# A gated feed-forward kernel: the low halves of the second weight chunk are made on TensorE and copied out by ScalarE

## The reference, cut to what matters

```python
# x (8, 512, 512), cond (8, 128), up_w (4096, 512), down_w (512, 2048), all float32
scale = cond @ norm_w.T + 1.0
ms = jnp.mean(x * x, axis=-1, keepdims=True)
h = x * (scale[:, None, :] * jax.lax.rsqrt(ms + EPS))
u = h @ up_w.T
val, gate = jnp.split(u, 2, axis=-1)
h = val * jax.nn.gelu(gate, approximate=False)
hq = act_quant(h)       # 127 / max|h| of each row, round, clip
wq = weight_quant(down_w)   # ternary, one scale
y = hq @ wq.T
return y + x
```

## Time and profile before

| | |
|---|---|
| median of 3 runs | 813.84 us (813.39 to 815.17) |
| profiled execution | 815.42 us; its span, first to last instruction, 813.6 us |
| TensorE busy | 773.3 us, 95% of the span |
| VectorE, ScalarE, GpSimd busy | 74%, 55%, 31% of the span |
| granted TensorE clock, mean | 0.981 of full |

### The profile page before, as it was taken

How to read it: one execution, slowest core, us unless ns; L and a number is a source line. 1 busy time by engine, 2 the same in 40 slices (tenths; PEclk the granted TensorE clock), 3 DMA queues, 4 the chain that set the end, 5 groups by cost and what they waited for, 6 DMA issues and landing times.

```text
span 813.6 us, 17562 instructions
## 1 busy us (share of the span) xinstructions
PE 773.3 (95%) x6401; PEld 637.2 (78%) x6401; DVE 603.5 (74%) x855; ACT 444.0 (55%) x1023; POOL 252.9 (31%) x314
## 2 busy tenths in 40 slices
PE   5898989899899999999999999999999999999987
PEld 4687878778668897789868887789778987888853
DVE  5897987869456895489756995489647995589577
ACT  5687767477533654355535655366535654455523
POOL 3876965357211232123211223123211232111100
PEclk9799999999899999999999999999999999999999
DMA  6435763836445154535455255525645345515512
GB/s 217 158 124 182 251 215 129 318 106 222 153 182 195 56 194 147 186 118 176 169 172 180 90 180 168 183 75 184 202 129 180 113 157 187 188 46 187 185 52 78
DMA packets 34507, 130.88 MB, mean 161 GB/s; under 512 B 3224, under 2 KB 3744, under 8 KB 34464
## 3 DMA queue, kind: packets, MB, share of 16 engines
q1 hardware_dynamic: 33920, 130.04, 47.1%
q10 hardware_dynamic: 544, 0.27, 0.1%
HBM read 110.89 MB, written 19.40 MB: 160 GB/s over the span
## 4 chain that ended last, share of the span: by engine, by line
PE 71%; DVE 6%; DMA 2%; ACT 1%; issue 1%; SPq 0%; DVEq 0%; ACTq 0%
PE A L1062 11%; PE A L1065 11%; PE A L1064 11%; PE Y L1114 11%; PE B L1065 8%; PE B L1062 8%; PE B L1064 8%; DVE h L843 2%; DMA xin<-in_x_dram 2%; PE X L1010 1%; DVE mpart L822 1%; DMA w_scratch<-wslots 1%; DVE h L809 1%; PE X L1102 1%; DVE q L848 1%
## 5 line engine op out<-in xcount | busy, mean ns | idle before, releaser
L1062 PE MATMUL A<-xT,wslots 128*128 (+1 forms) x1024 | 281.3, 275 | 15.5 <-ACT snapC L599 12.2
L1065 PE MATMUL A<-xT,wslots 128*128 (+1 forms) x1024 | 281.5, 275 | 0.0
L1064 PE MATMUL A<-xT,wslots 128*128 (+1 forms) x1024 | 281.4, 275 | 0.0
L496 POOL TENSOR_TENSOR snapC<-snapC 128x256 f32<-128x256 f32 x128 | 101.9, 796 | 494.6 <-ACT snapC L599 494.2
L1062 PE MATMUL B<-xT,wslots 128*128 (+1 forms) x768 | 210.7, 274 | 0.7 <-DVE h L803 0.7
L1064 PE MATMUL B<-xT,wslots 128*128 (+1 forms) x768 | 210.7, 274 | 0.0
L1065 PE MATMUL B<-xT,wslots 128*128 (+1 forms) x768 | 210.6, 274 | 0.0
L809 DVE SCALAR_TENSOR_TENSOR h<-h,c_all,g 128x512 f32<-128x512 f32 (+1 forms) x128 | 106.6, 833 | 127.0 <-ACT g L622 126.3
L1062 PEld LDWEIGHTS A<-xT,wslots 128*128 128x128 f16 x1024 | 100.8, 98 | 32.2 <-ACT snapC L599 14.1
L1064 PEld LDWEIGHTS A<-xT,wslots 128*128 128x128 f16 x1024 | 100.9, 99 | 14.7
L1065 PEld LDWEIGHTS A<-xT,wslots 128*128 128x128 f16 x1024 | 101.0, 99 | 12.4
(11 more groups left out here) (136 smaller groups left out, 936.9 us busy)
## 6 DMA issues: line engine op xcount, KB each, us to landing
wslots<-w_scratch SPq DMA_DIRECT2D x84, 896.0 KB, 4.7
w_scratch<-wslots SPq DMA_DIRECT2D x12, 896.0 KB, 4.6
wst<-in_L_cond_up_w_dram SPq DMA_DIRECT2D x16, 512.0 KB, 5.7
xin<-in_x_dram SPq DMA_DIRECT2D x8, 1024.0 KB, 7.3
dwb<-in_L_cond_down_w_dram SPq DMA_DIRECT2D x16, 512.0 KB, 4.6
wst<-in_x_dram SPq DMA_DIRECT2D x28, 256.0 KB, 5.5
out_dram<-wst SPq DMA_DIRECT2D x28, 256.0 KB, 5.1
xin<-in_x_dram SPq DMA_DIRECT2D x4, 256.0 KB, 4.0
```

The costliest lines, as they stand in the source:

```text
L496: pool.tensor_tensor(snapC[:, s % 2, 0:H], snapC[:, s % 2, 0:H], snapC[:, s % 2, H:T], ALU.add)\
L1062: pe.matmul(into, high, xh, start=(start and kp == 0), stop=False, skip_group_check=not start)
L1064: pe.matmul(into, high, xl, start=False, stop=False, skip_group_check=not start)
L1065: mm = pe.matmul(into, low, xh, start=False, stop=last, skip_group_check=not start)
```

## The change

The low halves of chunk 1 (S2 and S4) are now made the way those of chunk 0 were: `subtract_high(s+1, 1)` on TensorE, `w_low_first(s+1, 1)` on ScalarE, and VectorE's `w_low(s+1, 1)` is gone. The semaphores count accordingly: `wlo0_ready` now rises twice for each step and `wlo_ready` two times instead of three. No DMA, tile or bank is added.

```diff
-            def w_low_first(p):
+            def w_low_first(p, c):
-                act.wait_ge(wlo_psum, p + 1)
+                act.wait_ge(wlo_psum, 2 * p + c + 1)
...
@@ scalar, batch 0 @@
                 if s + 1 < FT:
-                    w_low_first(s + 1)
+                    w_low_first(s + 1, 0)
                     w_high(s + 1, 1)
                 if s > 0:
                     gelu_second(0, s - 1)
                 if s + 1 < FT:
+                    w_low_first(s + 1, 1)
                     w_high(s + 1, 2)
...
@@ vector, batch 0 @@
-                if s + 1 < FT:
-                    w_low(s + 1, 1)
                 if s > 0:
                     hidden(0, s - 1)
                     largest(0, s - 1)
...
@@ tensor @@
-            def subtract_high(p):
-                blk, n = W_CHUNKS[0]
-                pe.wait_ge(whi_ready, NC * p + 1)
+            def subtract_high(p, c):
+                blk, n = W_CHUNKS[c]
+                pe.wait_ge(whi_ready, NC * p + c + 1)
...
                 p2(0, s)
                 if s + 1 < FT:
+                    subtract_high(s + 1, 1)
                     transpose_w(s + 1, 2)
                 p7(0, s)
```

More of the change, by code:

```diff
@@ L350, in store_slot @@
             def store_slot(s):
-                sp.wait_ge(wlo0_ready, s + 1)
-                sp.wait_ge(wlo_ready, (NC - 1) * (s + 1))
+                sp.wait_ge(wlo0_ready, 2 * (s + 1))
+                sp.wait_ge(wlo_ready, (NC - 2) * (s + 1))
                 sp.dma_start(scratch[s - KEPT], wslots[:, slot_of(s), :]).then_inc(w_stored[(s - KEPT) % RING], 16)
@@ L589, in w_high @@
                 act.activation(w_part(p, 0, blk, n), WB[at % 3][:, 0:n * KP * P], ACT.Copy).then_inc(whi_ready, 1)
-            def w_low_first(p):
-                blk, n = W_CHUNKS[0]
-                act.wait_ge(wlo_psum, p + 1)
-                act.activation(w_part(p, 1, blk, n), WB[NC * p % 3][:, 0:n * KP * P], ACT.Copy).then_inc(wlo0_ready, 1)
+            def w_low_first(p, c):
+                blk, n = W_CHUNKS[c]
+                act.wait_ge(wlo_psum, 2 * p + c + 1)
+                act.activation(w_part(p, 1, blk, n), WB[(NC * p + c) % 3][:, 0:n * KP * P], ACT.Copy).then_inc(wlo0_ready, 1)
             def snap_u3(b, s):
@@ L680, in _ @@
             x_high(0, 1, 0)
-            w_low_first(0)
+            w_low_first(0, 0)
             w_high(0, 1)
             x_high(0, 0, 1)
+            w_low_first(0, 1)
             x_high(0, 1, 1)
@@ L944, in _ @@
             x_low(0, 1, 0, 2)
-            w_low(0, 1)
             x_low(0, 0, 1, 3)
@@ L1015, in low_done @@
                 p, c = divmod(at, NC)
-                if c == 0:
-                    pe.wait_ge(wlo0_ready, p + 1)
-                else:
-                    pe.wait_ge(wlo_ready, (NC - 1) * p + c)
-            def subtract_high(p):
-                blk, n = W_CHUNKS[0]
-                pe.wait_ge(whi_ready, NC * p + 1)
-                pe.matmul(WB[NC * p % 3][:, 0:n * KP * P], minus16[:, :], w_part(p, 0, blk, n), start=False, stop=True,
+                if c < 2:
+                    pe.wait_ge(wlo0_ready, 2 * p + c + 1)
+                else:
+                    pe.wait_ge(wlo_ready, (NC - 2) * p + c - 1)
+            def subtract_high(p, c):
+                blk, n = W_CHUNKS[c]
+                pe.wait_ge(whi_ready, NC * p + c + 1)
+                pe.matmul(WB[(NC * p + c) % 3][:, 0:n * KP * P], minus16[:, :], w_part(p, 0, blk, n), start=False, stop=True,
                           skip_group_check=True).then_inc(wlo_psum, 1)
@@ L1172, in _ @@
             transpose_w(0, 1)
-            subtract_high(0)
+            subtract_high(0, 0)
             transpose_w(0, 2)
+            subtract_high(0, 1)
             transpose_w(0, 3)
@@ L1192, in _ @@
                 if s + 1 < FT:
-                    subtract_high(s + 1)
+                    subtract_high(s + 1, 0)
                     transpose_w(s + 1, 1)
```

## The result

| | before | changed |
|---|---|---|
| median on the same chip, us | 813.97 (4 runs) | 842.76 (4 runs, 839.19 to 844.84) |
| ratio, with its 95% interval | | 1.035 [1.0325, 1.0374] |
| profiled execution, its span | 815.42, 813.6 | 839.19, 837.3 |
| granted TensorE clock, mean | 0.981 | 0.983 |

The changed kernel is 3.5% slower, 28.8 us by the medians and 23.7 by the profiled spans (its profiled execution is the fastest of the four). The forecast was no change. Ratios in this document leave out runs more than 1.5% above the fastest of their kernel, among them six single runs of 1099 to 4571 us (three of the kernel before, one each of e3, e6 and e8) that no profile explains; where that hides something else, the run is named.

The account below looks back on a forecast made before the run. TensorE, busy 95% of the span, was taken as the bound; added matmuls and copy remainders, less VectorE's shorter chains, gave +1.0 us on the 813.84 median: 814.8 us (813.8 if a half-rate stretch goes), range 812.6 to 817.4.

Parts of the forecast that it names:

- Nothing changed stands after 138.64, so the shift of that copy is the shift of the end.: End of batch 0: the shift of ScalarE's last chunk copy, at 138.64 us, was taken as the whole kernel's shift.
- Matmul, +0.22 in the row: TensorE, steps 0 to 14: each added 512-column matmul takes 0.22 us where TensorE runs through; 3.3 us for all 15.
- Copy on ScalarE, hidden but for 0.04: ScalarE, each step: the new copy's 0.48 us falls into an idle gap before chunk 2's copy, except for 0.04.
- Three waits for VectorE, 4.3 to 2.0 in total: Batch 0: TensorE's waits for low halves at 82.61, 104.90 and 127.32 shrink to about 0.6, 1.3 and 0.1 us.
- my chain: VectorE's `hidden`, then chunk 2's low halves, then TensorE: 0.2, 0.6 and 0.6 us sooner at 82.61, 104.90, 127.32.
- I had p4 there 1.3 us sooner once the stretch is gone: p4 at 111.40 in batch 0 would start 1.3 us sooner without the half-rate stretch from 106.2 to 109.5.
- The clock: After 104.90: the wait falls from 2.12 to about 1.3 us; losing the half-rate stretch behind it saves 1.0 us.
- The one behind 64 I had left where it was: TensorE's 2.09 us wait at 64.28 in batch 0 is not shortened, since ScalarE sets it.
- The sum, +1.0 or 0.0 at 138.64: End of batch 0: net shift +1.0 us at an unchanged clock, 0.0 without the half-rate stretch after 104.90.
- rivals 1 and 2: 1: TensorE pays all 15 matmuls in full, 817.3 us, chance 0.18; 2: ScalarE's copies find no gap, 821.0, chance 0.04.
- 3 or 4: 3: VectorE's relief and the clock, faster, 813.1 or 811.9 us, chance 0.12; 4: one half-rate stretch more, 816.1, chance 0.10.

Follow-up runs that it names:

- e3: Changed kernel with 64 idle wait instructions added at the start of TensorE's program, ahead of the loop: 817.7 us, ratio 1.0043.
- e6: Changed kernel with 64 idle instructions ahead of TensorE's loop, laid where TensorE stands idle anyway: 816.1 us, ratio 1.0023.
- e8: Kernel before with 16 idle instructions at the start of TensorE's program: median 814.44 us, ratio 0.9998; single runs up to 827.5.
- experiment 4: Kernel before with 16 or 48 idle instructions ahead of TensorE's loop: 814.44 and 856.76 us; also compared instruction packets ahead of costly and harmless returns across profiles.
- experiment 5: Changed kernel with TensorE's loop written out and without the added matmul, ScalarE's copy kept: 811.52 us, ratio 0.9972.
- e4: Changed kernel with TensorE's loop over batches 2 to 6 written out: 814.06 us, ratio 1.000.
- e13: Changed kernel with TensorE's loop written out, repeated on another chip: 812.07 us, ratio 0.9972.
- e17: Changed kernel with TensorE's loop written out, a third time: 813.56 us, ratio 0.9993.
- e5: Kernel before with TensorE's loop over batches 2 to 6 written out: 813.49 us, ratio 0.9994.
- e7: Changed kernel with only batch 2 written out ahead of TensorE's loop, leaving three returns: 837.24 us, ratio 1.0285.
- e10: Changed kernel with TensorE's loop written out and the added matmul left out, VectorE's relief and ScalarE's copy kept: 811.52 us, ratio 0.9972.
- e11: Kernel before with the change only at weight blocks 7, 10 and 13, TensorE's loop kept: 812.06 us, ratio 0.998.
- e15: Change only at weight blocks 7, 10 and 13, TensorE's loop kept, run once more: 818.17 us, ratio 1.0018.
- e16: Change only at weight blocks 7, 10 and 13, with TensorE's loop written out: 810.62 us, ratio 0.9951.
- e1: Kernel before with 32 idle instructions at the start of TensorE's program: 842.73 us, ratio 1.0363.
- e2: Kernel before with 96 idle instructions at the start of TensorE's program: 820.6 us, ratio 1.0081.
- e9: Kernel before with 64 idle instructions ahead of TensorE's loop, laid where TensorE stands idle anyway: 812.95 us, ratio 0.9996.
- e12: Kernel before with 48 idle instructions (+48) at the start of TensorE's program, two runs only: 856.76 us, ratio 1.0527.
- e14: Kernel before with TensorE's loop written out, repeated on another chip: 813.24 us, ratio 0.9993.

## Why the prediction was wrong

**The step that failed** is "Nothing changed stands after 138.64, so the shift of that copy is the shift of the end." No operation after it is changed, but the whole loop stands 32 instructions further along TensorE's stream, and its four returns then cost 6.6 us each. I counted the added instructions by their time and not by their place, and no rival had a term for it: 821.0 was the dearest. The page of the kernel before could have raised the question, since it holds a `q8 instruction` row, and the kernel a loop of which I never asked how it returns; it could not have given the answer, for the same loop is free there. What in the loop's place makes its returns costly stays open beyond the packets of experiment 4.

**The rest, by its own steps:**

- *Matmul, +0.22 in the row*: right (44.81 to 45.03). The figure of the Trainium skill (TensorE: Matmul & The Clock Gate, Back-to-back issue gap) that I set beside it, 131 ns, is for a sustained stream; the section's other one, about 216 ns for an isolated matmul of 512 columns, agrees with the 0.22 us of this trace. End to end the 15 cost 0 to 2.5 us (experiment 5), which can't tell 2.0 from the 3.3 of the rows, as part is hidden.
- *Copy on ScalarE, hidden but for 0.04*: right in step 2, where it starts at 45.23 and chunk 2's copy follows at 45.72, so released by ScalarE itself. Relative to TensorE's earlier shift of 0.17 it is 0.27 later, forecast 0.26.
- *Three waits for VectorE, 4.3 to 2.0 in total*: 1.9 in total, but divided otherwise: 1.07, 0.80 and none, against 0.6, 1.3 and 0.1. The third is covered by a wait for GpSimd's combinations (0.43 at 125.58), a releaser that my chain did not have. In e4, e13 and e17 they are 0.35, 0.80 and 0.93, 2.1 in total. Counted from the p4 ahead of each wait to its end, in those three profiles the first chain is 0.7 us shorter than before (2.04 against 2.72), the second 1.1 (9.04 against 10.14), the third 0.2 longer (16.16 against 15.92); I had 0.2, 0.6 and 0.6 shorter. That their sum comes out (1.6 against 1.4) is luck.
- *A new wait* at 110.32 of 1.26 us for ScalarE's snapshot was not forecast. ScalarE there waits 0.86 for VectorE's xT:

```profile
107.99 0.69 ACT L573 ACTIVATE xf<-X,scl 128x512 f32<-128x512 f32 x1 [0.86 <-DVE xT L764]
```

  The change alone does not make this wait: e5, with VectorE's subtraction and without the half-rate stretch ahead of it, has it too:

```profile
111.20 0.28 PE L1062 MATMUL A<-xT,wslots 128*128 128x256 f16 x1 [1.04 <-ACT snapC L599]
```

  I had p4 there 1.3 us sooner once the stretch is gone. From the end of TensorE's wait for VectorE to this p4 it is 6.50 us before (104.90 to 111.40), 6.06 in e5 and 6.47 in the changed kernel. So this term was too large: the full clock gives 0.4 us in e5, and TensorE spends the rest waiting for ScalarE.
- *The clock*: the half-rate stretch after the second wait is gone, as forecast, in every profile in which that chain is relieved (the changed kernel, e3, e4, e6, e7, e10, e11, e13, e15, e16, e17); of the eight kernels with VectorE's subtraction seven have it (before, e1, e2, e8, e9, e12, e14), e5 not. The one behind 64 I had left where it was. It follows the same wait of 2.1 to 2.4 us in 14 of the 19 profiles and not in the changed kernel's, e5, e6, e16 and e17, so it is no effect of the change. In the changed kernels batch 0 takes, from its first product to the copy of the last chunk, 115.9 us on average with it (e3, e4, e7, e13) and 114.6 without (after, e6, e17): 1.3 us of the profiled difference is chance.
- *The sum, +1.0 or 0.0 at 138.64*: -1.2 measured, but in a profile without that stretch. The four changed ones that have it take 115.1 to 116.3 us for batch 0, measured as above, the seven with the subtraction and both stretches 115.2 to 116.0: on average +0.4, against my 0.0. With the returns taken out the medians of the change are -1.2 to +0.6 us. As to batch 0 the forecast of no change holds, in part by the luck named above; rivals 1 and 2 (+3.5, +7.2) did not come, nor 3 or 4 as something that the medians show.

## What to carry to other kernels

An instruction added ahead of a hardware loop moves the loop in its engine's stream. Look at the `instruction` queue and at waits for issue at the loop's returns before and after; where they appear, write the loop out or shift it by instructions that do nothing, and only then judge the change. A change that relieves a waited-for engine pays at the places where somebody waits for it: doing it at 3 of 16 gained 0.4 to 0.5% in the one timing of e16, doing it at all 16 nothing that shows. And a median that leaves out outliers can hide a kernel that stands on such an edge; read the single runs.

## What the runs showed of the hardware

- A return of TensorE's loop of 1597 instructions is free or costs 6.6 us (with a longer second halt some 10 us, at +48), by where the loop stands; after a costly one 9 packets of 16 KB are fetched through the round, and a stretch at a granted 0.50 follows (344.5 to 347.9).
- Each costly return had a packet 1.0 to 3.4 us ahead of it, the harmless ones none or one 5.2 us and more ahead.
- Written out, the same batches fetch 6 packets each (51 in all in e4 and e5) and have no wait for issue there.
- A TensorE instruction that only waits on satisfied semaphores took 0.11 us (3.44 us for each further 32, e1, e3, e2).
- The same wait of 2.1 to 2.4 us of TensorE (near 64 us) was followed by a granted 0.50 in 14 of 19 profiled executions and by full clock in five.
